# A weight ring in SBUF fed from one DMA queue, or from two: half 0 from SyncE, half 1 from ScalarE

## What is computed

```
fl = LN(patches of x)                       # 64 patches (tokens) of 1024
pf = merge(softmax(q k) v + dwconv(v)) @ Wout_p      # q, k = fl @ Wqk_p,  v = fl @ Wv_p
ww = softmax(LN(pooled) @ Wqk_w ...)        # 4 windows
wv = heads(LN(windows of x) @ Wv_w)         # Wv_w:   16384 x 1024, float32
wf = merge(nds @ wv + dwconv(wv)) @ Wout_w  # Wout_w: 1024 x 16384, float32
out = x + diag_scaled * pf + wf
```

## Time and profile before

| | before |
|---|---|
| median of 3 runs | 751.72 us (751.68 to 752.82) |
| the profiled execution | 752.75 us, its span 751.0 us |
| PE busy / ACT busy / DVE busy | 449.7 / 38.0 / 91.4 us |
| data moved by DMA | 320.57 MB, 427 GB/s over the span |
| share of SP's queue q1 of the 16 DMA engines' span | 98.8% |
| chain of work that ended last | DMA 59%, PE 35%, DVE 4%, ACT 1% |

### The profile page before, as it was taken

One profiled execution on the slowest core, in us unless ns is written; L12 is line 12 of the kernel. 1 busy time (PEld: TensorE's weight loads), 2 busy tenths in 40 slices (PEclk: granted clock), 3 DMA queues, 4 the chain that ended last, 5 costly groups with the idle time before them and its releaser, 6 DMA issues.

```text
span 751.0 us, 6989 instructions
## 1 busy us (share of the span) xinstructions
PE 449.7 (60%) x3076; PEld 144.3 (19%) x3076; DVE 91.4 (12%) x254; ACT 38.0 (5%) x79; POOL 9.3 (1%) x21
## 2 busy tenths in 40 slices
PE   6699944444446455455487987544544565555557
PEld 5334200000002111111122342000000121111113
DVE  4756200000002000000006071000000020000000
ACT  2111100000000000000001020000000000000000
POOL 2100000000000000000001000000000000000000
PEclk9589967777777777777787999677777778778779
DMA  9999999999999999999999999999999999999996
GB/s 390 444 397 442 437 444 422 436 426 447 433 426 429 443 430 429 426 443 436 414 442 440 415 431 442 437 436 429 440 429 436 429 440 427 436 433 433 429 420 253
DMA packets 7496, 320.57 MB, mean 427 GB/s; under 512 B 1001, under 2 KB 1281, under 8 KB 1721
## 3 DMA queue, kind: packets, MB, share of 16 engines
q1 hardware_dynamic: 7397, 320.12, 98.8%
q10 hardware_dynamic: 84, 0.23, 0.1%
HBM read 319.86 MB, written 0.49 MB: 427 GB/s over the span
## 4 chain that ended last, share of the span: by engine, by line
DMA 59%; PE 35%; DVE 4%; ACT 1%; issue 1%; SPq 0%; DVEq 0%; ACTq 0%
DMA ring<-halves 59%; PE bank L501 11%; PE bank L473 10%; PE bank L391 4%; PE bank L400 2%; PE bank L408 1%; PE bank L300 1%; PE bank L457 1%; PE bank L525 1%; DVE conv_p L820 1%; PE bank L371 1%; PE bank L318 0%; DMA cst<-blurs 0%; DVE ring L692 0%; PE bank L362 0%
## 5 line engine op out<-in xcount | busy, mean ns | idle before, releaser
L473 PE MATMUL bank<-ring,stage 128*4 128x512 f32 x1024 | 142.2, 718 | 144.5 <-DMA ring<-halves 144.5
L501 PE MATMUL bank<-ring,wf_t 128*32 128x512 f32 x1024 | 146.9, 738 | 115.8 <-DMA ring<-halves 115.8
L501 PEld LDWEIGHTS bank<-ring,wf_t 128*32 128x32 f32 x1024 | 35.7, 132 | 215.2 <-DMA ring<-halves 118.5
L473 PEld LDWEIGHTS bank<-ring,stage 128*4 128x4 f32 x1024 | 27.1, 97 | 259.3 <-DMA ring<-halves 158.3
L300 PE MATMUL bank<-ident,area 128*128 128x128 f32 (+1 forms) x234 | 32.8, 287 | 14.3 <-ACT area L624 11.8
L905 DVE TENSOR_TENSOR image<-bank,image 128x32 f32 (+1 forms) x30 | 5.1, 194 | 273.8 <-PE bank L300 273.8
L870 DVE COPY wv_t<-bank 128x32 f32<-128x32 f32 x2 | 0.4, 191 | 292.4 <-PE bank L300 292.4
L300 PEld LDWEIGHTS bank<-ident,area 128*128 128x128 f32 (+1 forms) x234 | 28.5, 193 | 33.4 <-ACT area L624 25.4
L624 ACT COPY area<-bank 128x512 f32<-128x512 f32 x15 | 8.8, 585 | 279.5 <-PE bank L501 279.5
L391 PE MATMUL bank<-extra,area 128*64 128x512 f32 x64 | 18.9, 757 | 1.9 <-DVE area L779 1.9
L457 PE MATMUL bank<-extra,area 128*64 128x512 f32 x64 | 15.9, 653 | 1.9 <-DVE area L844 1.9
(11 more groups left out here) (197 smaller groups left out, 200.6 us busy)
## 6 DMA issues: line engine op xcount, KB each, us to landing
ring<-halves SPq DMA_DIRECT2D x5, 4096.0 KB, 22.4
extra<-ends SPq DMA_DIRECT2D x4, 4096.0 KB, 17.3
ring<-halves SPq DMA_DIRECT2D x1, 2048.0 KB, 26.1
ring<-halves SPq DMA_DIRECT2D x2, 1024.0 KB, 28.7
ring<-halves SPq DMA_DIRECT2D x33, 29.5
ring<-images SPq DMA_DIRECT2D x1, 512.0 KB, 3.6
area<-window_gains SPq DMA_DIRECT2D x1, 256.0 KB, 13.2
windows_last<-area SPq DMA_DIRECT2D x1, 256.0 KB, 2.0
```

The lines of the kernel that those rows point to most:

```text
L473: m = mm(bank[0][32 * j:32 * j + 4, :], stage[:, k // 8, at:at + 4], w[:, j], start=False, stop=False)
L501: m = mm(bank[6 + g][32 * j:32 * j + 32, :], wf_t[:, h, :], w[:, j], start=(h == 0 and onto is None), stop=(h == GROUP - 1))
```

## The change

The loads of half 1 of the ring for turns 1 to 7 of layer 0 and turns 1 to 6 of layer 1 are taken out of SP's loop and issued by ACT, into ACT's queue. SP keeps half 0, `extra`, all loads up to turn 0 of each layer, and the last turn of layer 1. ACT waits for the same count of `slots_used` as SP did. In the `Wv_w` turns its load stands behind the stage copy of half 1, in the `Wout_w` turns behind `copy_group(i, 1)`.

```diff
@@ SP
                 with sp.Fori(1, 2 * TURNS - L) as t:
-                    for b in range(2):
-                        sp.wait_ge(slots_used, t * TURN + (used(L, S_VW) + b * HALF - HALF))
-                        load_half(L, t, b)
+                    sp.wait_ge(slots_used, t * TURN + (used(L, S_VW) - HALF))
+                    load_half(L, t, 0)
@@ ACT
-                with act.Fori(0, TURNS) as i:
-                    for half in range(2):
-
-                        act.wait_ge(slots_used, i * TURN + (used(L, S_VW) + 8 * half - 8))
-                        sc.copy(stage[:, half, :], area[2][:, bass.ds(i * 128 + 64 * half, 64)]).then_inc(staged, 1)
+                def load_second(t):
+                    act.dma_start(half_of_ring(1), half_of_weights(L, t, 1)).then_inc(half_landed[1], 16)
+
+                def copy_stage(i, half):
+                    act.wait_ge(slots_used, i * TURN + (used(L, S_VW) + 8 * half - 8))
+                    sc.copy(stage[:, half, :], area[2][:, bass.ds(i * 128 + 64 * half, 64)]).then_inc(staged, 1)
+
+                for half in range(2):
+                    copy_stage(0, half)
+                with act.Fori(1, TURNS) as i:
+                    copy_stage(i, 0)
+                    copy_stage(i, 1)
+                    load_second(i)
+                act.wait_ge(slots_used, used(L, S_OUTW))
+                load_second(TURNS)
@@
-                with act.Fori(0, TURNS - L) as i:
-                    for g in range(2):
-                        copy_group(i, g)
+                with act.Fori(0, TURNS - 1 - L) as i:
+                    copy_group(i, 0)
+                    copy_group(i, 1)
+                    load_second(i + (TURNS + 1))
+                for g in range(2):
+                    copy_group(TURNS - 1 - L, g)
```

More of the change, by code:

```diff
@@ L218, in slot_of, with half_of_ring, half_of_weights @@
             return ring[:, at:at + SLOT]
+        def half_of_ring(b, lo=0, hi=HALF):
+            return ring[:, (b * HALF + lo) * SLOT:(b * HALF + hi) * SLOT]
+        def half_of_weights(L, t, b, lo=0, hi=HALF):
+            return halves[t * 2 + (L * N_HALVES + 2 + b)][:, lo * SLOT:hi * SLOT]
         def used(L, s):
@@ L248, in load_half @@
             def load_half(L, t, b, lo=0, hi=HALF):
-                sp.dma_start(ring[:, (b * HALF + lo) * SLOT:(b * HALF + hi) * SLOT],
-                             halves[t * 2 + (L * N_HALVES + 2 + b)][:, lo * SLOT:hi * SLOT]).then_inc(half_landed[b], 16)
+                sp.dma_start(half_of_ring(b, lo, hi), half_of_weights(L, t, b, lo, hi)).then_inc(half_landed[b], 16)
             for L in range(2):
```

## The result

| | before | changed |
|---|---|---|
| median of 5 runs | 752.4 us (751.7 to 752.8) | 792.6 us (783.0 to 795.5) |
| ratio, 95% interval | | 1.0505 (1.0481 to 1.0528) |
| the profiled execution | 752.75, span 751.0 | 783.01, span 781.3 |
| DMA share, 5 to 740 us | 1.00 | 0.97 |

The forecast was 766 us, in a range of 753.5 to 779. Measured is 40 us more than before where 14 were forecast, which lies above the range. The direction was right, and so was the sharing behind it; the size was not. Executions of the kernels with two queues differ by 3 to 23 us from one to the next, those of the kernel before by up to 2, so medians and intervals count here, and the profiled execution of the changed kernel was the fastest of its five. A ratio leaves out the executions that took over 1.5% longer than the fastest of their kernel (here one, of 795.5 us).

The account below looks back on a forecast made before the run. The prediction took the DMA engines, full from 5 to 740 us, to bound the kernel. Dry turns 13 plus seam 1 made 14 us: 752.75 + 14 - 1.0 = 766 us, forecast 762 to 778, 80% range 753.5 to 779.

Parts of the forecast that it names:

- What bounds the kernel: Whole kernel: DMA engines are full between start and tail, so every microsecond they stand dry is added to the time.
- Sharing row by row: Turns: two queued half-loads share the engines by rows of 2.4 us, half the rate each; half 0 lands about 7 us late.
- The rival without sharing: Turns and seam: queues alternate load by load, nothing is dry, time 751.7 us; chance 14%.
- The dry spell of a turn: Each turn: engines stand dry when half 1's remaining load is shorter than the 10.9 us for half 0's next load.
- served by whole rows, the older load ends up to a row earlier: Turns: correction to fluid sharing; half a row (1.2 us) earlier on average, shrinking each dry spell by that.
- the 5.2 us a layer: Turns: dry time per layer with service by whole rows, 0 + 0.6 + 2.3 + 2.3 + 0 + 0.
- The fluid 22.0: Turns of both layers: dry time with sharing treated as a fluid, 11.0 us a layer; high end for the turns.
- Restart after a dry spell: Turns: getting the engines going again after standing dry; the prediction gave it no term of its own.
- The seam: Between the layers: next layer's first extra load runs beside half 1's; 0 to 4.4 us dry, 1 taken.
- ScalarE's side costs nothing: ScalarE's issuing: a load takes 0.33 us to issue, ScalarE has idle time before its copies, so no cost of its own.
- nearer the row-wise value: Sum for the turns: 13 us taken between 10.4 and 22.0, raised a little for the last of sixteen staggered engines.
- The cold second burst: Turns: clock falls in the 2.5 us gap, second burst takes 9.4, turns never dry; 753.4 to 758 us; chance 12%.

Follow-up runs that it names:

- rows16k_two: The changed kernel with every half loaded by four transfers of 2 slots, rows of 16 KiB, in both queues: 788.9 us, ratio 1.0498.
- delay_1: The changed kernel with one dummy copy on ScalarE (about 0.6 us) ahead of each load of half 1: 782.8 us, ratio 1.0322.
- after: The changed kernel itself, first profile, nothing further changed: median 792.6 us, ratio 1.0505; profiled execution 783.01 us.
- after_again: The changed kernel run once more, unaltered, for a second profile: 790.8 us in one execution.
- after_same_chip: The changed kernel, unaltered, run beside other experiments on the same chip: 793.5 us, ratio 1.0541.
- rows16k_seam_delay: The changed kernel with 16 KiB rows in both queues, SP waiting at the seam and one dummy copy ahead of each ScalarE load: 775.2 us, ratio 1.0225.
- rows16k_one: The kernel before, all loads from SP, with every half loaded by four transfers of 2 slots, rows of 16 KiB: 759.7 us, ratio 1.0092.

## Why the prediction was right and wrong, point by point

**What bounds the kernel: right.** The dry spells and the slow first rows behind them account for 29.5 of the 30.3 us.

**Sharing row by row: right.** Half 0 landed at 131.7 in turn 1 (131.5 had been worked out), half 1 at 143.8 (143.4), and q10 carried 109.28 MB. Bursts come in pairs. The rival without sharing is refuted for these loads: in the packet records, put together engine by engine, rows of q1 and q10 alternate one by one on all sixteen engines, from 116.5 us until half 0's last row in turn 1 and in the same way in turn 2, each row taking 2.42 us (median).

**The dry spell of a turn: the correction had the wrong sign.** The step that failed is "served by whole rows, the older load ends up to a row earlier". The opposite holds. The DMA queues of the changed kernel from 171.2 to 173.3 us:

```profile
DMA packets 13, 0.85 MB, mean 406 GB/s; under 512 B 0, under 2 KB 0, under 8 KB 0
...
q10 hardware_dynamic: 13, 0.85, 93.9%
```

Half 0's load (q1) has moved its last row by 171.1 and starts no packet in this stretch, yet it lands only at 173.8. In the packet records its last semaphore writes, at 173.4 and 173.5, stand right behind a row of q10 that began at 170.9 and 171.1, where q1's last row on that engine had ended: the write came one row of the other queue later. The writes also spread from 166.4 to 173.5 over the sixteen engines, whose records show two rows of half 1 ahead of the writes before 167, three ahead of those from 168.9 to 170.1 and four ahead of the last two, and PE waits for the last; before, they spread over 1.8 us. Even sharing, worked out as in the prediction but from the issues as they were (SP's at 140.47, ACT's at 152.92), would land half 0 near 170, an estimate; with the issues of `rows16k_two` near 169. Measured are 173.8 and 168.6. So here the older load of coarse rows ends some 4 us later than even sharing has it, not a row earlier; the 5.2 us a layer had no ground.

The fluid 22.0 for the two layers stands against 21.4 measured in the first profile, 29 and 34 in the other two. That the first two agree is luck, as layer 1's cold second bursts (below) made up for layer 0's longer spells: by layer it is 16.4 and 5.0 where the sum has 11.0 twice, and ahead of the loads of turns 3 to 7 of layer 0 it is 3.1, 4.7, 4.9, 2.4 and 1.4 us where the sum has 1.8, 3.5, 3.5, 1.1 and 1.1. The steady spell, worked out as 3.5, was 4.7 in turn 3: half 1 had 6.4 us left after half 0's landing, not 6.9, and half 0's burst took 10.0 us from PE's start to the reload's issue, not 9.4. Over the three profiles the spells that had built up were 4.0 to 5.4 us, in both matrices. In the Wout turns 1.1 was forecast and 1.4 to 5.3 measured; a turn inherits the cover of the one before, while the sum treated each as settled at once.

**Restart after a dry spell: missing from the sum**, which put it at nothing without saying so. The slow first rows come to 7 to 8 us in each of the three profiles.

**The seam: right in size, 1.1 us against 1 taken, and in part by luck.** The sum took seam and turns as independent. The kernels whose turns ahead were not dry had 10 to 14 us there (`delay_1`, `rows16k_two`), and in `rows16k_two` the 14 lie where the 0 to 4.4 had been worked out. The second load of `extra` came at 444.02, 24.7 us after its 419.28 of before, where 1 to 10 had been written; 16.4 of these are the dry spells of layer 0.

**ScalarE's side costs nothing: right.** In `delay_1` 0.7 us more on each of its loads did not cost time either.

**The sum.** By row: turns 13 taken, 21 to 34 measured; seam 1 and 1.1; restarts 0 and 7.5; the tail 0 and -1.5. Two steps failed. The larger is the choice of 13 "nearer the row-wise value": even the lowest measured 21.4 is 8 us more. The other is the restarts at nothing, 7.5 us, for which the range's upper end of 779 had no room. For the median of 40 us, rather than this execution's 30, the turns' 29 to 34 stand, which no value in the prediction reached. The DMA share from 100 to 740 us was 0.96, where 0.97 to 0.99 had been written.

**The cold second burst: a rival with 12%, and it came in part.** The sum had the second burst of turn 1 warm, 7.3 us; in layer 0 it took 8.75, after a gap of 3.61 us in which the granted clock stayed at 1.00, and the clock was 0.67 from 143.9 to 147.0. In turns 2 to 6, with hardly a gap, it took 7.05 to 7.07, and there the turns ran dry. In the Wv turns of layer 1 of the first profile it was cold three times (10.01, 8.39 and 8.75 us after gaps of 2.87 to 3.49), and those turns were nearly free of dry spells, as the rival says. In the other two profiles the burst of turn 1 was warm after the same gap, and they were not. The prediction took one clock for all turns; it differs from layer to layer and from one execution to the next.

## What to carry to other kernels

Here one queue kept the DMA engines full (a share of 1.00 from 5 to 740 us), and its order was worth something: in turns 1 to 3 of layer 0 a load took 28.7 to 29.8 us from issue to landing, against 33 to 37 for half 0's beside the other queue, and the next load waited behind it as cover. Splitting alternate loads over two queues added no bandwidth here (414 GB/s from 5 to 740 us, against 432) and made the first of two finish late and the second close behind it, which cost 5%. If two queues must be used, let them carry loads that are not each other's cover; that is an inference, and nearest to it comes the run in which the queues met only at the first turn and the seam (1.0074). Look in the table of stretches for a DMA share below 1.00 and on PE's timeline for bursts in pairs.

No form was faster than the kernel before. The nearest was the one with all turn loads in ACT's queue (1.0074). With a DMA share of 1.00 from 5 to 740 us, the kernel before leaves nothing to gain there by the order of the loads.

## What the runs showed of the hardware

- In the changed kernel an engine took rows of 64 KiB from q1 and q10 by turns, 2.42 us each (median), and half 0's last completion writes came after one more row of q10 (no packet of q1 starts from 171.2 to 173.3, the last write is at 173.5, landing at 173.8).
- After a dry spell the first row of 64 KiB on an engine mostly took 3.0 to 3.5 us instead of 2.42 (`after`, `after_again`, `after_same_chip`).
- A half in four transfers with rows of 16 KiB instead of one with rows of 64 KiB, on one queue, cost 7 us of 753 (1.0092).
- With rows of 16 KiB in both, two queues moved what one did: 428 GB/s in `rows16k_seam_delay`, 429 in `rows16k_one` from 480 to 740 us.
